# A Mamba block with adaLN modulation: modulations made as columns, filler matmuls on TensorE, a new order of the first projections, and the last ffn in quarters

## The reference

```
mod = silu(c) @ wmod              # c: 2 x 512; mod: 2 x 6 x 512
sa, ca, ga, sb, cb, gb = the six parts;  ga, gb = sign * max(abs, 0.25)
h = layernorm(x) * (1 + ca) + sa
x = x + ga * mamba(h)
h = layernorm(x) * (1 + cb) + sb
x = x + gb * (sum over r of h @ factors[r] / sqrt(8) + bias)

mamba(h): h, gate = split(h @ in_proj.T)          # 1024 channels each
          h = silu(causal conv of 4 taps along the rows)
          dt, B, C = split(h @ x_proj.T)          # 128, 16, 16
          dt = softplus(dt @ dt_proj.T + b)
          state = state * exp(dt * A) + dt * h * B   # per channel, 16 states, along the rows
          y = sum over states of state * C + h * D
          return (y * silu(gate)) @ out_proj.T
```

## Time and profile before

| | |
|---|---|
| three runs | 1928.4, 1929.47, 1930.35 us |
| median | 1929.47 us |
| the profiled execution | 1929.0 us, of which the span of instructions is 1927.3 us |
| granted TensorE clock over the span, mean | 0.975 |
| first scan starts (L1548) | 54.30 us |
| busy share of the span | PE 89%, PEld 68%, DVE 93%, ACT 80%, POOL 93% |

### The profile page before, as it was taken

How to read it: one execution, slowest core, us unless ns; L and a number is a source line. 1 busy time by engine, 2 the same in 40 slices (tenths; PEclk the granted TensorE clock), 3 DMA queues, 4 the chain that set the end, 5 groups by cost and what they waited for, 6 DMA issues and landing times. The chain is left out here.

```text
span 1927.3 us, 29502 instructions
## 1 busy us (share of the span) xinstructions
PE 1720.6 (89%) x9176; PEld 1311.1 (68%) x9176; DVE 1801.3 (93%) x2260; ACT 1546.2 (80%) x4529; POOL 1794.0 (93%) x756
## 2 busy tenths in 40 slices
PE   7995998989899998998989899998989989899798
PEld 4664767667576766767677676766768676676664
DVE  3897999999999999999999999999999999999995
ACT  3776789798888979888787988879788897988773
POOL 1899999999999999999999999999999999999993
PEclk9897999999999999999999999999999999999899
DMA  5756514032140412304042340503213041321310
GB/s 179 258 115 157 145 51 163 24 128 82 55 143 20 152 50 100 110 23 164 23 153 66 116 148 23 165 23 137 72 72 127 34 152 35 104 78 44 111 28 33
DMA packets 72077, 186.17 MB, mean 97 GB/s; under 512 B 6896, under 2 KB 8560, under 8 KB 63984
## 3 DMA queue, kind: packets, MB, share of 16 engines
q1 hardware_dynamic: 68224, 176.94, 27.1%
q0 software_dynamic: 3696, 7.34, 2.4%
HBM read 172.20 MB, written 12.06 MB: 96 GB/s over the span
## 5 line engine op out<-in xcount | busy, mean ns | idle before, releaser
L604 POOL TENSOR_TENSOR ub<-u,b_all 128x2048 f32<-128x2048 f32 x255 | 1166.8, 4576 | 40.7 <-DMA b_all<-bc_scratch 40.7
L756 ACT ACTIVATE decay<-dt,decay_rate 128x256 f32<-128x256 f32 x2048 | 883.7, 465 | 20.4 <-DVE state_p L1548 1.1
L1548 DVE TENSOR_TENSOR_SCAN decay<-decay,ub 128x512 f32<-128x512 f32 x617 | 729.1, 1212 | 21.7 <-ACT decay L756 16.1
L620 POOL TENSOR_TENSOR sc_p<-state_p,c_all 128x1024 f32<-128x1024 f32 (+1 forms) x256 | 499.8, 1952 | 53.1 <-PE y_bank L1088 31.6
L1548 DVE TENSOR_TENSOR_SCAN state_p<-decay,ub 128x512 f32<-128x512 f32 x407 | 480.1, 1207 | 34.5 <-ACT decay L756 32.1
L1088 PE MATMUL y_bank<-ident,sc_d 128*128 128x128 f32 x2468 | 364.6, 279 | 103.6 <-DVE sc_d L1563 103.5
L1088 PEld LDWEIGHTS y_bank<-ident,sc_d 128*128 128x128 f32 x2468 | 289.0, 143 | 180.8 <-DVE sc_d L1563 127.4
L1563 DVE TENSOR_TENSOR sc_d<-decay,c_all 128x512 f32<-128x512 f32 x617 | 395.5, 675 | 7.4 <-PE y_bank L1088 1.7
L742 ACT ACTIVATE carry<-decay 128x2 f32<-128x2 f32 x617 | 99.8, 162 | 220.4 <-DVE sc_d L1563 219.0
L1170 PE MATMUL bank_a<-hT,win_h 128*128 128x256 f32 x992 | 236.3, 384 | 15.3 <-DVE hc L1612 7.8
L1088 PEld LDWEIGHTS y_bank<-ident,sc_p 128*128 128x128 f32 x1628 | 195.6, 145 | 65.5 <-issue 33.2
(11 more groups left out here) (137 smaller groups left out, 1813.3 us busy)
## 6 DMA issues: line engine op xcount, KB each, us to landing
win_h<-win_m SPq DMA_DIRECT2D x128, 256.0 KB, 2.6
win_z<-win_m SPq DMA_DIRECT2D x128, 256.0 KB, 2.7
b_all<-bc_scratch SPq DMA_DIRECT2D x31, 1024.0 KB, 4.7
c_all<-bc_scratch SPq DMA_DIRECT2D x31, 1024.0 KB, 5.1
xa<-x SPq DMA_DIRECT2D x16, 512.0 KB, 5.1
xc<-x SPq DMA_DIRECT2D x16, 512.0 KB, 3.8
out<-xc SPq DMA_DIRECT2D x15, 512.0 KB, 3.7
ffn<-factors POOLq DMA_DIRECT2D x7, 1024.0 KB, 10.1
```

The source lines that it names most:

```text
L604: pool.tensor_tensor(ub[:, slot, :, :, :], u[:, (PAIRS * c + q) % U_PAIRS, :, :].unsqueeze(1).to_broadcast([P, QUAD, 2, ROWS]), b_all[:, n ...
L620: pool.tensor_tensor(sc_p[:, slot:slot + k, :, :], state_p[:, slot:slot + k, :, :], c_all[:, n:n + k, :].unsqueeze(2).to_broadcast([P, k, ...
L756: last = act.activation(bk[:, j * ROWS:(j + 1) * ROWS], dt[:, pair % DT_PAIRS, j, :], ACT.Exp, scale=decay_rate[:, e, n:n + 1])
L1548: dve.tensor_tensor_scan(dst, bk[:, :], ub[:, quad % UB_RING, i, :, :].rearrange("p j r -> p (j r)"), 0.0, ALU.mult, ALU.add).then_inc(sca ...
```

## The change

- `row_mods` and `turn_mods` become `column_mods(j)`: now a 128x128 block of wmod is stationary and the two columns of the silu of c move. That is 16 products (32 matmul instructions, each with a weight load of 128 columns) for each j, straight into the 128x2 columns. `copy_mod_rows` goes. `copy_mods(2, SB)` and `(3, CB)` move from step 3 to step 1.
- `warm_up(n)`: n products of the identity with itself into y_bank (2n instructions of 128 columns): 12 at TensorE's start, 2 behind `column_mods(1)`, 8 behind the last `project_out_last`.
- In chunk 0 the tanh of odd pairs goes into a part of `skipped`, so a tanh waits for the silu two pairs back.
- `copy_dt(0)` goes ahead of `copy_bc(0)`. On TensorE both `project_dt` of pairs 2 and 3 go ahead of `project_b_c(0, 2)`, `expand_dt(0, 0)` goes ahead of `project_b_c(0, 3)`, both `spread_b` follow, then `expand_dt` 1 and 2; `expand_dt(0, 3)` goes into step 1, behind that step's transposes.
- `soft_dt(0, 1)` moves from ahead of the first scan to step 2.
- The last ffn waits for each 128x128 of the modulation by itself.

```diff
-            copy_bc(0)
             copy_dt(0)
+            copy_bc(0)
             soft_dt(0, 0)
-            soft_dt(0, 1)
...
                     if c == 0 and s == 2:
+                        soft_dt(0, 1)
                         soft_dt(0, 2)
                         soft_dt(0, 3)
...
+            def warm_up(times):
+                for _ in range(times):
+                    pe.matmul(y_bank[:, 0:P], ident[:, :], ident[:, :], start=True, stop=True)
...
-                for k in range(KD):
-                    last = pe.matmul(bank_c[i][0:BATCH, :], cond_h[:, k, :], staged[i][:, k, :],
-                                     start=(k == 0), stop=(k == KD - 1))
+                for m in range(KD):
+                    for k in range(KD):
+                        last = pe.matmul(bank_c[i][:, m * BATCH:(m + 1) * BATCH], staged[i][:, k, m * P:(m + 1) * P], cond_h[:, k, :],
+                                         start=(k == 0), stop=(k == KD - 1))
                 last.then_inc(stage_used[i], 1)
...
+            pe.wait_ge(consts_made, 1)
+            warm_up(WARM)
             pe.wait_ge(prep, 2)
-            row_mods(0)
+            column_mods(0)
             pe.wait_ge(consts_made, 2)
             turn_x(0, 0)
             turn_x(0, 1)
-            row_mods(1)
-            turn_mods(0)
-            turn_mods(1)
+            column_mods(1)
+            warm_up(WARM_H)
...
-            for q in range(2, PAIRS):
-                project_b_c(0, q)
-                project_dt(0, q)
+            project_dt(0, 2)
+            project_dt(0, 3)
+            project_b_c(0, 2)
+            expand_dt(0, 0)
+            project_b_c(0, 3)
             spread_b(0)
-            expand_dt(0, 0)
+            spread_b(1)
             expand_dt(0, 1)
-            spread_b(1)
             expand_dt(0, 2)
-            expand_dt(0, 3)
-            row_mods(2)
-            row_mods(3)
+            column_mods(2)
+            column_mods(3)
...
-                        if s == 2:
-                            turn_mods(2)
-                            turn_mods(3)
+                        if s == 1:
+                            expand_dt(0, 3)
...
+            warm_up(WARM_L)
             for t in range(LB):
                 pe.wait_ge(c_free[t], c_jobs + 1)
                 spread_bias(t, BATCH - 1)
                 turn_z_last(t)
             for t in range(LB):
-                pe.wait_ge(h2_made, t + 1)
                 for k in range(KD):
+                    pe.wait_ge(h2_made, KD * t + k + 1)
```

More of the change, by code:

```diff
@@ L44 @@
 DVE_TAPS = 1
+WARM, WARM_H, WARM_L = 12, 2, 8
 PE_TAPS = range(DVE_TAPS, TAPS - 1)
@@ L271, in build @@
         warm = sb("warm", [P, 1])
-        mod_row = [hc[0:BATCH, 2 * j:2 * j + 2, :].rearrange("p k r -> p (k r)") for j in range(2)]
         spare = [hT[i][:, :, :].rearrange("p k r -> p (k r)").rearrange("p (t d) -> p t d", t=2) for i in range(H_RING)]
-        mod_row += [spare[2][0:BATCH, j, :] for j in range(2)]
         staged = [y_rows[:, :, :].rearrange("p t e -> p (t e)").rearrange("p (k d) -> p k d", k=KD),
@@ L320, in build @@
         consts_made, rate_exp, cond_tanh, prep = sem("consts_made"), sem("rate_exp"), sem("cond_tanh"), sem("prep")
-        bias_scaled, mods_copied, mods_turned = sem("bias_scaled"), sem("mods_copied"), sem("mods_turned")
+        bias_scaled = sem("bias_scaled")
         b_spread, b_first, c_first = sem("b_spread"), sem("b_first"), sem("c_first")
@@ L333, in h_lane, with tanh_lane @@
             return bank_c[q % 2] if c == 0 and q >= 2 else bank_a[q % 2]
+        def tanh_lane(c, q):
+            return skipped[:, 0, :, :].rearrange("p j r -> p (j r)") if c == 0 and q % 2 else tanh_s[:, :]
         def rows_of(view, c):
@@ L828, in tanh_before @@
                     act.wait_ge(c_free[1], C_JOBS * (c - 2) + 2)
-                if q:
-                    act.wait_ge(a_free[(q - 1) % 2], A_FREES * c + 2 + (q - 1) // 2)
-                act.activation(tanh_s[:, :], h_lane(c, q)[:, :], ACT.Tanh).then_inc(tanh_h_made, 1)
+                if q >= (2 if c == 0 else 1):
+                    before = q - 2 if c == 0 else q - 1
+                    act.wait_ge(a_free[before % 2], A_FREES * c + 2 + before // 2)
+                act.activation(tanh_lane(c, q), h_lane(c, q)[:, :], ACT.Tanh).then_inc(tanh_h_made, 1)
             def skip(c, q):
@@ L973, in _ @@
             act.activation(warm[:, :], ident[:, 0:1], ACT.Softplus)
+            copy_dt(0)
             copy_bc(0)
-            copy_dt(0)
             soft_dt(0, 0)
-            soft_dt(0, 1)
             act.wait_ge(prep, 5)
@@ L1063, in _ @@
                 for k in range(KD):
-                    made = act.activation(hT[(FINAL + 1) % H_RING][:, k, t * P:(t + 1) * P], bank_a[t][:, k * P:(k + 1) * P], ACT.Identity,
+                    act.activation(hT[(FINAL + 1) % H_RING][:, k, t * P:(t + 1) * P], bank_a[t][:, k * P:(k + 1) * P], ACT.Identity,
                                           bias=mods[:, SB, k, BATCH - 1:BATCH],
-                                          scale=mods[:, CB, k, BATCH - 1:BATCH])
-                made.then_inc(h2_made, 1)
+                                          scale=mods[:, CB, k, BATCH - 1:BATCH]).then_inc(h2_made, 1)
         @block.tensor
@@ L1340, in spread_b, with column_mods @@
                 last.then_inc(b_spread, 1)
-            def row_mods(j):
+            def column_mods(j):
                 i = j % 2
@@ L1611, in silu_before @@
                 wait_u(dve, PAIRS * (c - 1) + q + 1)
-                dve.scalar_tensor_tensor(out=hc[:, 2 * q:2 * q + 2, :].rearrange("p k r -> p (k r)"), in0=tanh_s[:, :],
+                dve.scalar_tensor_tensor(out=hc[:, 2 * q:2 * q + 2, :].rearrange("p k r -> p (k r)"), in0=tanh_lane(c, q),
                                          scalar=1.0, in1=h_lane(c, q)[:, :], op0=ALU.add,
@@ L1671, in copy_mods @@
             def copy_mods(i, kind):
-                dve.wait_ge(mods_turned, i + 1)
+                dve.wait_ge(stage_used[i % 2], i // 2 + 1)
                 dst = mods[:, kind, :, :].rearrange("p k b -> p (k b)")
@@ L1675, in copy_mods @@
                 dve.tensor_scalar(dst, bank_c[i % 2][:, 0:KD * BATCH], one, None, ALU.add).then_inc(mods_made, 1)
-            def copy_mod_rows(i):
-                dve.wait_ge(stage_used[i % 2], i // 2 + 1)
-                dve.tensor_copy(mod_row[i], bank_c[i % 2][0:BATCH, :]).then_inc(mods_copied, 1)
             def sign_rows(i, gates):
@@ L1714, in _ @@
             shifts(0, mv_a, nrm_a, norm_a)
-            copy_mod_rows(0)
-            copy_mod_rows(1)
             copy_mods(0, SA)
@@ L1758, in one_round @@
                         if s == 1:
-                            copy_mod_rows(2)
-                            copy_mod_rows(3)
-                        if s == 3:
                             copy_mods(2, SB)
```

## The result

The changed kernel takes 1934.34 us (median of 9 runs, 1931.80 to 1936.94) against 1929.47 (9 runs, 1927.52 to 1931.70): ratio 1.0024, 95% interval 1.0014 to 1.0034. It is 4.9 us slower. The profiled execution took 1933.76 us, its span is 1932.0: 4.7 more than before's. Two executions far slower than the rest are left out of every comparison: one of 9431 us in e11, and one of 2039 us of the kernel before, beside e5 to e8.

The account below looks back on a forecast made before the run. The prediction took DVE and POOL, both 93% busy, to share the bound, with DVE's arrival at 111 us deciding. 1929.0 + 2.6 + 5.9 - 0.7 - 1.9 = 1934.9; 0.5 to the median, given as 1935 us; range 1923 to 1939.

Parts of the forecast that it names:

- steps 3 to 6: Chunk 0 after step 2: no turning or row copies, mod_rows(4) moves with the scans; -0.7 us, from -2 to +1.
- the way to the first scan: First modulation to first scan: tanh's own buffer, new order and moved softplus give -0.85 us, from 0 to -1.7.
- step 2: Last softplus waits for expand_dt(0, 3) behind column_mods(2) and (3) at falling clock; DVE +5.9 us, from +0.8.
- a narrow product: One column_mods instruction, 128-column weight load with two columns moving: 0.22 us at 1.2 GHz, 0.11 at 2.4.
- head, at the first modulation: column_mods(0) and (1) at 1.2 GHz start ACT's modulation 2.5 us later; +2.6 with projections, from -4.6 to +3.5.
- sixth scan, in all: DVE's lateness at its sixth scan in chunk 0: the head's +2.6 and step 2's +5.9 us together.
- behind POOL's wait: From POOL's wait at 111 us to the tail: everything moves with DVE's arrival there, no further term.
- tail: Last ffn starts 0.9 us earlier and takes 7.0 us at 2.4 GHz thanks to filler; -1.9 us, -0.4 to -2.1.
- The clock: TensorE in column_mods: narrow products neither bring the clock up nor hold it, so most run at 1.2 GHz.
- Rival A: The clock holds through the column products, as 128-row weights count: -4.9 us, 1924.5 us; chance 0.28.
- rival B: DVE makes up some 3.5 of step 2's 5.9 us in existing waits before 111 us: 1931.5 to 1932; chance 0.22.
- The softplus's own cost: In step 2, softplus for three pairs, not two (+0.85 us); with the clock at 2.4 GHz, DVE +0.8 against before's clock.

Follow-up runs that it names:

- e11: e1 run again, beside e12: the changed kernel with 128 columns moving in all column products; 1923.10 us, ratio 0.9969 to the kernel before.
- e5: The changed kernel with 128 columns moving only in column_mods(0) and (1), 2 in (2) and (3); 1926.69 us, ratio 0.9994 to the kernel before.
- e8: The kernel before with the last ffn in quarters and no filler in the tail; 1928.27 us, ratio 1.0004.
- e1: The changed kernel with 128 columns moving in place of 2 in the column products, same weight loads; 1922.39 us, ratio 0.9972 to the kernel before.
- e4: The kernel before with only the tail's edits, 8 filler products and the ffn in quarters; 1926.28 us, ratio 0.9991.
- e12: e1 with soft_dt(0, 1) back ahead of the first scan, expand_dt(0, 1) ahead of spread_b, expand_dt(0, 3) ahead of column_mods(2); 1921.36 us, ratio 0.9961 to the kernel before.

## Why the prediction was right

The forecast was 1935, the measurement 1934.34, and it is the forecast's own mechanism: the clock in the columns, and the last softplus behind them. That the number is this close is in part luck. Between the profiled executions the forecast was +5.9 us and the traces show +4.8: steps 3 to 6 were 1.4 too dear and the way to the first scan 0.5, and against that stood 0.3 too little in step 2 and 0.5 that no step had. Step by step, forecast against the trace of the change:

| step | forecast | measured |
|---|---|---|
| a narrow product, low and high clock | 0.22, 0.11 us | 6.83 / 32 = 0.21; 3.5 us for 32 = 0.11 |
| head, at the first modulation | +2.5 (+2.6 with the projections' clock) | +2.66 |
| from there to the first scan | -0.85 | 1.34 - 2.66 = -1.32 |
| sixth scan, in all | 2.6 + 5.9 = +8.5 | +8.39 |
| steps 3 to 6 | -0.7 | 6.29 - 8.39 = -2.10 |
| behind POOL's wait, up to the last output products | 0 | about +0.5 |
| tail | -1.9 | 4.77 - 6.78 = -2.01 |

(6.78 is 1912.28 against 1905.50.)

*The clock* was the step on which all turned, and the row on which it rested had weights of 2 rows where the new ones have 128. e1 and e11 settle it: with the same 128 rows of weights the clock stays up or comes back once 128 columns move, so the width that moves decides, not the rows of the weights. Which widths between 2 and 128 would do was not tried. Rival A's mechanism does not happen by itself; e1 is what it would have been, 1922.4, where the forecast for it was 1924.5. The rule for a weight load's time in the Trainium skill ("TensorE: Matmul & The Clock Gate", section "LDWEIGHTS (loading the stationary operand)") has no clock in it; here 32 loads of 128 columns take 3.7 us at 1.00 and 6.95 at 0.50, so the measurement decides against it.

*Steps 3 to 6* are the term that was mis-sized, by 1.4 us. Two waits of DVE were there to be given back: 1.98 at `sign_rows`, now 0.98, and one of 1.5 us for the turned modulations in step 3, which the change does away with:

```profile
71.09 0.17 DVE L1675 TENSOR_SCALAR mods<-bank_c 128x8 f32<-128x8 f32 x1 [1.54 <-PE bank_c L1357]
```

The forecast counted one microsecond for both and then gave 0.3 back to a clock that had in fact risen again by 79.9 us. This is rival B's mechanism in small: it gave 2.1, not 3.5. POOL stayed behind DVE: 2.81 and 2.19 us of wait at the two places (3.47 and 2.16 before), so the lateness went through unchanged.

*The softplus's own cost* was hidden in a sum that came out right. Forecast between first and sixth scan with the clock up was 0.8 + 0.85 = 1.65; e11 has 2.3. Behind it stands `expand_dt(0, 3)`, which can't start before the second softplus has freed its bank.

*The tail* was right in both parts, and e4 and e8 bear out the split, more sharply than forecast: quarters alone -0.2, with the filler -2.3, as far as overlapping intervals can. From the last output products to the end of the ffn it is 16.56 us in the change and in e4, and 18.58 before. The tail does not test the sentence of the Trainium skill that a transpose doesn't count as TensorE's activity in the same way ("TensorE: Matmul & The Clock Gate", "Part 4: PE-mode transpose"). Between the filler's end and the ffn lie 2.4 us, of transposes and pauses, and at the head of the kernel before the clock was still up after 2.3 us with no work at all (20.91 to 23.23). What speaks against the sentence is still the stretch from 71.7 to 74.8 in the kernel before, transposes alone ahead of the rise.

*Behind POOL's wait* came some 0.5 us that no step had, and they came within chunk 0: DVE's scan at 134.76 us in the kernel before is 6.15 late, the one at 142.28 is 6.82 late, and chunk 1 starts 6.83 late (195.95 against 189.12). e4, whose head is that of the kernel before, loses 0.8 us between the same two scans. So it need not be the change's doing; it may lie in the one profiled execution of the kernel before. At the first scans of chunks 1 to 15 the lateness is between 6.5 and 7.7 us. In the profiled execution of e12 the gain shrank from 7.5 us at the end of chunk 1 to 4.8 at the last chunk. From chunk 2 on, a chunk of 64 units takes 114.1 us between first scans in most places, 114.8 in some, and down to 113.2 in the middle; the stretches of low clock lie elsewhere in each execution and kernel. That one brings the other was not tried.

## What to carry to other kernels

A matmul that is busy by the profile can still leave TensorE at 1.2 GHz: read the granted clock over each stretch of narrow products, not the busy share. Where a 128-column weight load sets the pace anyway, let as many columns move as the load hides (here 128, at no time of its own); it turned a 4.9 us loss into a 6 us gain. And before a step is moved behind a block of another engine's work, ask what that block takes at the lower clock, and which buffer ties the moved step to the one ahead of it.

## What was not expected of the hardware

The same 32 weight loads took 6.83 us with 2 columns moving and 3.74 us with 128. Wide columns raised the clock while they ran (e11, 0.50 to 1.00 at 11.3 us); narrow ones, shown just as busy, did not in 15 us. Filler products on idle TensorE can matter for what runs behind them: with 16 instructions of it in the tail the ffn took 7.03 us in every trace, without them 8.15 once and 7.36 once. What the 24 at the start are worth, some 2 us by the medians, the intervals and the traces leave open.
